# Attention tower: softmax sums of twelve heads in one PSUM area, inverted once per image

## What is computed

```python
qkv = fake_quant(x, sx1, zx1) @ fake_quant(ww1, sw1, zw1).T
q, k, v = map(split_heads, jnp.split(qkv, 3, axis=-1))
dots = jnp.einsum('bhnd,bhmd->bhnm', fake_quant(q, sq, zq), fake_quant(k, sk, zk)) * scale
a = jax.nn.softmax(dots, axis=-1)
out = jnp.einsum('bhnm,bhmd->bhnd', fake_quant(a, sa, za), fake_quant(v, sv, zv))
out = out.transpose(0, 2, 1, 3).reshape(B, N, HEADS * DIM_HEAD)
return fake_quant(out, sx2, zx2) @ fake_quant(ww2, sw2, zw2).T + bb2
```

## Time and profile before

| | us |
|---|---|
| median of three runs | 1542.82 |
| lowest, highest | 1542.39, 1545.75 |
| profiled execution | 1546.79 |
| its span in the trace | 1544.7 |
| DVE busy in the span | 1318.9 (85%) |
| PE busy | 1227.4 (79%) |
| ACT busy | 994.9 (64%) |

### The profile page before, as it was taken

One profiled execution on the slowest core, in us unless ns is written; L12 is line 12 of the kernel. 1 busy time (PEld: TensorE's weight loads), 2 busy tenths in 40 slices (PEclk: granted clock), 3 DMA queues, 4 the chain that ended last, 5 costly groups with the idle time before them and its releaser, 6 DMA issues.

```text
span 1544.7 us, 42798 instructions
## 1 busy us (share of the span) xinstructions
PE 1227.4 (79%) x11806; PEld 763.3 (49%) x11806; DVE 1318.9 (85%) x3249; ACT 994.9 (64%) x2005; POOL 420.0 (27%) x540
## 2 busy tenths in 40 slices
PE   5999966988888888888888888888864777667676
PEld 5999963444444444444444444444432434333343
DVE  4555781699999999999999999998996999999997
ACT  0000004578777787777877777877853888888886
POOL 7333450010000000000000000001023666666664
PEclk9999985599999999999999999998985766877875
DMA  7899951233333433334343433433331222222222
GB/s 246 261 276 281 307 178 41 71 113 119 112 118 114 121 115 117 113 118 119 112 121 109 123 115 112 122 109 109 117 114 52 77 82 83 85 78 86 81 83 65
DMA packets 154935, 192.01 MB, mean 124 GB/s; under 512 B 40208, under 2 KB 117072, under 8 KB 154576
## 3 DMA queue, kind: packets, MB, share of 16 engines
q1 hardware_dynamic: 99120, 154.10, 33.4%
q10 hardware_dynamic: 55776, 37.45, 8.3%
HBM read 156.99 MB, written 34.50 MB: 124 GB/s over the span
## 4 chain that ended last, share of the span: by engine, by line
PE 41%; DVE 28%; issue 16%; ACT 7%; DMA 4%; ACTq 3%; DVEq 1%; SPq 1%; POOL 0%
PE psum L1073 9%; PE psum L1190 7%; DVE pi L942 7%; PE psum L1130 5%; DVE qkb L795 5%; PE psum L1178 4%; PE psum L1137 4%; PE psum L1212 4%; DVE pT L795 3%; DVE big L1031 2%; ACTq L472 2%; ACT xT L522 2%; PE psum L1147 2%; DVE zti L917 2%; DVE oo L1048 1%
## 5 line engine op out<-in xcount | busy, mean ns | idle before, releaser
L942 DVE TENSOR_TENSOR pi<-big 128x788 int16<-128x788 f32 (+1 forms) x384 | 382.0, 995 | 0.0
L564 ACT ACTIVATE big<-psum 128x788 f32<-128x788 f32 (+1 forms) x384 | 316.1, 824 | 0.5 <-PE psum L1178 0.3
L708 POOL TENSOR_TENSOR h<-hin,att 128x192 f32<-128x192 f32 (+1 forms) x128 | 81.9, 641 | 859.1 <-ACT att L540 859.1
L1130 PE MATMUL psum<-xT,w1b 96*128 96x197 bf16 x1536 | 185.6, 259 | 43.8 <-ACT xT L522 43.8
L526 ACT ACTIVATE qki<-psum 128x394 int16<-128x394 f32 x384 | 181.7, 497 | 56.1 <-PE psum L1130 54.3
L1190 PE MATMUL psum<-big,sa_cols 128*32 128x197 f32 (+1 forms) x3072 | 216.6, 355 | 0.6 <-DVE zt L907 0.6
L1073 PE MATMUL psum<-big 128*128 128x192 f32 (+1 forms) x1200 | 198.4, 331 | 19.4 <-DVE big L753 16.9
L1073 PEld LDWEIGHTS psum<-big 128*128 128x128 f32 (+1 forms) x1200 | 196.5, 191 | 20.4 <-DVE big L753 16.9
L1178 PE MATMUL psum<-qkb 64*128 64x197 bf16 (+1 forms) x1536 | 140.6, 263 | 64.9 <-DVE qkb L795 64.9
L795 DVE TENSOR_SCALAR pT<-pi,lo,hi 128x788 bf16<-128x788 int16 (+1 forms) x384 | 179.9, 469 | 7.3
L1212 PE MATMUL psum<-winb,zT 96*128 96x512 bf16 (+1 forms) x396 | 153.7, 558 | 34.5 <-DVE big L1031 33.7
(11 more groups left out here) (104 smaller groups left out, 2074.2 us busy)
## 6 DMA issues: line engine op xcount, KB each, us to landing
big<-z_row SPq DMA_DIRECT2D x192, 394.0 KB, 3.4
big<-xt SPq DMA_DIRECT2D x98, 384.0 KB, 4.3
tin<-h_att SPq DMA_DIRECT2D x49, 192.0 KB, 2.4
tres<-h_att ACTq DMA_DIRECT2D x49, 192.0 KB, 2.5
out<-oo ACTq DMA_DIRECT2D x49, 192.0 KB, 2.6
h_res<-hp ACTq DMA_DIRECT2D x96, 96.0 KB, 3.9
hin<-h_res SPq DMA_DIRECT2D x64, 96.0 KB
h_att<-h SPq DMA_DIRECT2D x64, 96.0 KB
```

Of the source, the lines that this page charges most:

```text
L564: act.activation(ex[0:r, U1 * par + u, :, :].rearrange("p (a h) n -> p a h n", a=2), psum[0:r, 2 * (u % 2):2 * (u % 2) + 2, 0:2 * N] .rear ...
L942: v.tensor_tensor(pi[0:r, t, :, 0:N], ex[0:r, w % U1 + U1 * ((par + w // U1) % 2), :, :], zb[0:r, g, :, :], ALU.mult).then_inc(s_pi, 1)
L1130: last = mm(psum[:, bank, j * N:(j + 1) * N], w1b[:, c, ch:ch + 128], xT[:, c, :], start=(c == 0), stop=(c == 1))
```

## The change

All twelve heads' sums of an image accumulate in the same PSUM area. The constant column becomes sa_hot, three matrices of 32 columns with sa in column g only: the matmuls of group g add the sums of head j to partition 32j + g and zero to the others. The accumulation starts with the image's unit 0 and ends with its unit 5, which PE does in unit 0 of the next step. DVE turns, inverts (three columns) and turns back once per image, in its unit 1 of the next step. SP issues the three row writes together, then the h2 store and hin load, then the three broadcasts. To give the inverse time, the multiply moves from 7 to 11 units behind and the clip from 8 to 12; the o and y products, the ob and vb clips, POOL's add, and the store and load of h2 and hin move back with them, and one more step stands at the end. Line numbers of DVE and later code fall by one to three. The lines of the diff that set this:

```diff
-        zinv = sb("zinv", [128, 3, NZ], fp32)
-        sa_cols = sb("sa_cols", [128, 32], fp32)
+        zinv = sb("zinv", [128, NZ], fp32)
+        sa_hot = sb("sa_hot", [128, 3, 32], fp32)
...
-        SLOTS = [[("v", 3, 0), ("o", 1, -2), ("xt", 0, 1)],
-                 [("qk", 0, 1), ("qk", 1, 1), ("v", 0, 1)],
-                 [("o", 2, -2), ("qk", 2, 1)],
+        SLOTS = [[("v", 3, 0), ("o", 2, -3), ("xt", 0, 1)],
+                 [("qk", 0, 1), ("qk", 1, 1)],
+                 [("o", 0, -2), ("qk", 2, 1), ("v", 0, 1)],
                  [("qk", 3, 1), ("qk", 4, 1), ("qk", 5, 1)],
-                 [("o", 0, -1), ("y", 0, -2)],
-                 [("y", 1, -2), ("v", 1, 1), ("v", 2, 1)]]
+                 [("o", 1, -2), ("y", 0, -3)],
+                 [("y", 1, -3), ("v", 1, 1), ("v", 2, 1)]]
...
-        TT_LAG, CLIP_LAG = 7, 8
+        TT_LAG, CLIP_LAG = 11, 12
...
             def image_step(b, par):
-                nxt = 1 - par
-                spread(b, 0)
...
                 if exists(b, 2):
 
                     wait_apart(sp, full["xt"], b + 1)
                     load_xq(b + 2, par)
-                spread(b, 4)
+                if has_unit(b, -U1):
+
+                    wait_apart(sp, s_zinv, b)
+                    for g in range(3):
+                        wait_apart(sp, s_zb[g], 16 * (b - 1))
+                        sp.dma_start(z_row[g, :, :], zinv[g:128:32, 0:N]).then_inc(s_zrow[g], 16)
+                if has_unit(b, -2 * U1):
+
+                    wait_apart(sp, s_h2, 2 * b - 6)
+                    if has_unit(b, -4 * U1):
+                        store_h2(b - 4, par)
+                    for t, (t0, r) in enumerate(TOK):
+                        sp.dma_start(hin[0:r, par, t, :], h_res[bass.ds(b - 2, 1), t0:t0 + r, :]
+                                     .rearrange("a n d -> (a n) d")).then_inc(s_hin[par], 16)
+                if has_unit(b, -U1):
+                    for g in range(3):
+                        wait_apart(sp, s_zrow[g], 16 * b)
+                        wait_apart(sp, s_pi, 6 * (b - 2) + 2 * g + 2)
+                        sp.dma_start(zb[:, g, :, :].rearrange("p h n -> p (h n)"),
+                                     z_row[g, :, :].rearrange("h n -> (h n)").partition_broadcast(128))\
+                          .then_inc(s_zb[g], 16)
...
-                    summed = u % 2 == 0 and has_unit(b, u - 2)
+                    summed = u == 1 and has_unit(b, -U1)
...
-                        v.reciprocal(zti[:, :, 0], zt[:, :, 0]).then_inc(s_zti, 1)
...
+                        v.reciprocal(zti[:, :, 0:3], zt[:, :, 0:3]).then_inc(s_zti, 1)
...
                         for j in range(4):
-                            last = mm(psum[32 * j:32 * j + 32, 4, 0:N], sa_cols[0:r, :], ex[0:r, w % U1 + U1 * ((par + w // U1) % 2), j, :],
-                                      start=(w % 2 == 0), stop=(w % 2 == 1))
-                        if w % 2 == 1:
+                            last = mm(psum[32 * j:32 * j + 32, 4, 0:N], sa_hot[0:r, w // 2, :],
+                                      ex[0:r, U1 * ip + w, j, :], start=(w == 0), stop=(w == 5))
+                        if w == 5:
                             last.then_inc(s_zsum, 1)
```

More of the change, by code:

```diff
@@ L360, in over_images @@
         def over_images(eng, step):
-            for b in range(-1, 3):
+            for b in range(-1, 5):
                 step(b, b % 2)
[L365 to L368, removed]
+            with eng.Fori(0, (B - 8) // 2) as i:
+                step(2 * i + 5, 1)
+                step(2 * i + 6, 0)
+            for b in range(B - 3, B + 3):
                 step(b, b % 2)
@@ L701, in image_step @@
             def image_step(b, par):
[L702 to L705, removed]
+                if has_unit(b, -3 * U1):
+                    nxt = 1 - par
+                    wait_apart(pool, s_hin[nxt], hin_count(b - 3, nxt))
+                    if not isinstance(b, int) or b > 4:
+                        wait_apart(pool, s_h2st[nxt], h2_count(b - 3, nxt))
                     for t, (_, r) in enumerate(TOK):
-                        pool.wait_ge(evac["y"], 2 * b - 3 + t)
-                        nc.gpsimd.tensor_tensor(h2[0:r, par, t, :], hin[0:r, par, t, :], att[0:r, t, :], ALU.add)\
+                        pool.wait_ge(evac["y"], 2 * b - 5 + t)
+                        nc.gpsimd.tensor_tensor(h2[0:r, nxt, t, :], hin[0:r, nxt, t, :], att[0:r, t, :], ALU.add)\
                             .then_inc(s_h2, 1)
@@ L791, in _ @@
             const(v.memset(zti[:, :, :], 0.0))
-            const(v.tensor_copy(sa_cols[:, :], col(sc, SA).to_broadcast([128, 32])))
+            const(v.memset(sa_hot[:, :, :], 0.0))
+            for g in range(3):
+                const(v.tensor_copy(sa_hot[:, g, g:g + 1], col(sc, SA)))
             def clip(dst, src, s, r, which):
@@ L914, in image_step @@
                     if summed:
-                        dve.wait_ge(s_zt, G + 1)
-                        wait(dve, s_zinv, G)
-                        v.reciprocal(zti[:, :, 0], zt[:, :, 0]).then_inc(s_zti, 1)
[L918 to L925, removed]
+                        dve.wait_ge(s_zt, b)
+                        wait(dve, s_zinv, b - 1)
+                        v.reciprocal(zti[:, :, 0:3], zt[:, :, 0:3]).then_inc(s_zti, 1)
+                    if u == 1 and has_unit(b, -U1):
+                        dve.wait_ge(evac["v"], 4 * b)
+                        wait(dve, full["o"], 3 * (b - 2))
+                        clip(vb[:, nxt, :, :], vi[:, nxt, :, :], None, 128, ZV).then_inc(s_vb, 1)
+                    if u == 3 and has_unit(b, -3 * U1):
+                        dve.wait_ge(evac["o"], 3 * b - 6)
+                        wait(dve, full["y"], 2 * b - 6)
+                        clip(ob[:, :, 0:N], oi[:, nxt, :, :], None, 128, ZX2).then_inc(s_ob, 1)
                     if u in (3, 4) and exists(b, 1):
@@ L932, in image_step @@
                     if summed:
-                        dve.wait_ge(s_zti, G + 1)
-                        wait(dve, s_zrow[g], 16 * (b - 1 if u == 0 else b))
-                        v.transpose(zinv[:, g, :], zti[:, :, :].rearrange("p a b -> p (a b)")).then_inc(s_zinv, 1)
+                        dve.wait_ge(s_zti, b)
+                        for g in range(3):
+                            wait(dve, s_zrow[g], 16 * (b - 1))
+                        v.transpose(zinv[:, :], zti[:, :, :].rearrange("p a b -> p (a b)")).then_inc(s_zinv, 1)
                     if has_unit(b, u - TT_LAG):
```

40 lines of the change are left out of this document (10 added, 30 removed).

## The result

The changed kernel takes 1559.28 us (median of four runs, 1557.45 to 1567.25) against 1542.84 of the kernel before (1542.39 to 1545.75): a ratio of 1.0112, interval 1.0075 to 1.015. It is slower by 1.1%, where I forecast 1496 us and gave slower 0.07. The profiled execution took 1557.45 us, its span is 1555.3.

A forecast was written before the change was run, and what follows sets the result against it. DVE was taken to set the 13.84 us step; a 12.8 us loop would replace it, saving 61 us over 59 steps, with 10 added at start and end: 51 off 1546.8 gives 1496 us, range 1457 to 1535.

The forecast's parts named there:

- 59 x (13.84 - 12.8) = 61 us less: Attention steps: each of 59 falls from 13.84 to 12.8 us, saving 61 us before start and end are added.
- the ring: ACT's 12 exponential units: each exponential now waits for the multiply DVE does in its unit just before; costed at nothing.
- the other case: If ACT's 2.0 us of spare time were gone, one wait of 0.97 us per step would cost 57 us.
- PE's floor: PE's least time per step without its qkb and pT waits: 11.5 us work plus 0.7 waiting for xT, 12.2.
- DVE's relief: Two of three turn, reciprocal, turn groups on DVE go, at 0.86 us each: 1.72 us less per step.
- The long loop: The inverse's round per image, from DVE's turn through SP's rows and broadcast to the next turn: step floor of 12.8 us.
- The page's rule on engine counts: 69-row store and load halves would sit on three DMA engines and delay the broadcast; at z_row's delay, landing is 4.4 us.
- The start: Start-up at half clock, with y products beginning one step later: +4 us, bounds -1 to +9.
- The end: From the last image's first exponential to ob's last clip: 34.8 us in place of 28.6, +6 us.
- PE sets the step: Rival: broadcast lands in 3.4 us or less, PE bounds the step at 12.2, total 1458 us; chance 0.24.
- The slower rival: Store and load each delay the broadcast by 1.04 us; it lands at 5.5, step 14.3, total 1584 us; chance 0.07.
- The signs that I had named: 64 turns of each kind, step 12.8, DVE 85% busy and waiting for the broadcast, landing near 4, qkb and pT waits nearly gone.

The follow-up runs named there:

- the filler: Changed kernel with nine overwritten matmuls of 197 columns added on PE ahead of its wait for ACT's read of xT: 1493.61 us, ratio 0.9632.
- SP's new order: Changed kernel with SP's h2 store and hin load moved behind the first two broadcasts, the third behind them: 1448.3 us, ratio 0.935.
- SP order with the copy: Changed kernel with store and load behind the first two broadcasts, plus an ACT copy of 400 columns ahead of the xT read: 1628.64 us, ratio 1.0497.
- the DVE add: Kernel before with one DVE add of 480 float32 columns ahead of the second qkb clip, lengthening PE's wait for qkb: 1669.3 us, ratio 1.0819.

## Why the prediction was wrong

**The step that failed** is the sum "59 x (13.84 - 12.8) = 61 us less". It takes all 59 steps at the full clock because the steady stretch of the kernel before had it, and never says so: I read the clock column of rows 1 as a property of the stretch, not as something that hangs on the length of PE's waits. The chip gave 15 falls, 15 x 5.3 = 80 us, against a gain of 59 x (13.84 - 12.53) = 77. The difference of forecast and profile, 1557.45 - 1496 = 61 us, is this term: 59 x (13.88 - 12.8) = 64.

**The link that I mis-sized** is the ring: "ties ACT to DVE in every unit ... I cost it at nothing". ACT had the spare time, so the 57 us that I named for the other case never came. But the wait did, 0.34 to 0.42 in the steps shown (15 times in the 29 steps from 400 to 800 us, up to 0.9), and it went on into PE's wait for xT, which had been 0.69 and became 1.06 there, and up to 1.83 elsewhere. I had that wait in PE's floor ("11.5 + 0.7") and took it as fixed, although the change makes ACT late just ahead of it.

**What held.**
- DVE's relief: 1.72 us per step forecast. DVE's busy time fell from 1318.9 to 1214.9, 1.6 us for each of 64 images. The wider reciprocal takes 0.28 for 0.19, at no cost.
- The long loop: 12.8 forecast, 12.50 in the step shown and 12.53 over the 43 steps at full clock, 12.59 in the step shown with the filler. The issue of the first broadcast came at 6.3 us, as worked out; its data were used 3.7 later (4.0 taken). The median of 4.4 is over three broadcasts issued back to back, and the later two aren't waited for.
- The page's rule on engine counts, taken from the Trainium skill, "DMA: Bandwidth & Descriptors", section "Why a DMA increments its semaphore by 16 and not by 1", spoke for a broadcast delayed by the 69-row halves. The landing rose from 3.4 to 4.4 behind them and was 4.0 with two of three ahead of them, which agrees with it in sign; no run isolates the engine counts. The formula of 2.0 us plus bytes / 436 GB/s, from the same page of the Trainium skill, stands there in the section on DMAs that the gpsimd path issues; these are issued by SP, and the measured 3.4, which the sum used, was the better guide.
- The start: +4 forecast, 324.37 - 320.57 = 3.8. The end: +6 forecast. The last clip of ob, which answers to rows 10, stands 34.3 behind the last image's first exponential, 5.6 more than the 28.6 of before:

```profile
1177.45 0.59 DVE L794 TENSOR_SCALAR ob<-oi,lo,hi 128x1182 bf16<-128x1182 int16 x1 [1.55 <-ACT oi L541]
```

**The rivals.** "PE sets the step" at 12.2 describes the kernel with SP's new order (12.17) and not this one, where DVE waits for the broadcast at full clock. The slower rival forecast the right sign by a mechanism that did not happen: it needed a landing of 4.9 for the broadcast waited for, and that one took 3.7. None of them had the clock in it.

The signs that I had named: 64 turns, DVE waiting for the broadcast and the waits for qkb and pT gone all came. DVE is busy 81% of the steady stretch (323 of 400) in place of 85. "If ACT waits for pi, my zero for it was wrong" came too; it was the only one that pointed at the loss.

## What to carry to other kernels

Before forecasting a gain on a stretch at full clock, list PE's waits per step with their lengths and ask which of them the change makes longer: here 0.4 us more, and at times 1 us more, on one wait of 0.7 cost 5.3 us every fourth step, and ate a gain of 77 us while PE's idle time in all was more than halved. When a clock row turns from nines to eights, don't look for the idlest engine but for the one wait just ahead of each fall (here always the same one), and shorten it or fill it. A broadcast that everyone waits for belongs ahead of the store and load that nobody waits for.

## What the runs showed of the hardware

The granted clock fell from 2.4 to 1.2 GHz behind short waits of PE. One wait of 0.95 to 1.83 us in a step of 12.5, on a PE 93% busy, had a fall behind it in 15 of 59 steps, and one of 1.15 in 26 of 59 (SP order with the copy), where the other 33 waits of the same length had none. The kernel before, with 2.2 us per step in three waits of up to 1.08, had one fall in 59 steps. In the steady stretch the clock then stayed down 13.7 us each time, though PE was busy without a pause in it (13.40 of 13.40 us in the window shown); it was 17.1 us for one of the two falls with the filler, and 17 to 21 with the DVE add. High load is not a cause: 98% busy ran at 1.00 for 400 us, 84% at 0.90.

The Trainium skill, page "TensorE: Matmul & The Clock Gate", section "A second HAM failure mode: psum-queue depth-cycling", describes a kernel whose clock swings between both levels because PE pauses briefly and often between groups of matmuls. The trace agrees, and adds the sizes: pauses of mostly 0.9 to 1.8 us once per step, 4.2 to 5.7 us lost for each fall.

Why the xT place tolerates less than the qkb place (six falls behind waits of 0.87 against none behind waits of up to 1.08) stays open. So does which steps are hit: the wait of 1.04 before 702.74 was followed by no fall, that of 1.06 before 715.24 was.
